# Position bias: the first layer of odd groups as table sums on GpSimd, with half the position columns

## What is computed

```python
pos = grid_q[:, :, None, :] - grid_kv[:, None, :, :]       # 1024 queries x 64 keys x (x, y)
bias = jnp.sign(pos) * jnp.log1p(jnp.abs(pos))
bias = jax.nn.relu(bias @ cpb_w1 + cpb_b1)                 # 2 -> 128
bias = jax.nn.relu(bias @ cpb_w2 + cpb_b2)                 # 128 -> 128
bias = (bias @ cpb_w3 + cpb_b3).reshape(b, GROUPS, H * W, Hd * Wd)   # 128 -> 1
```

## Time and profile before

| | us |
|---|---|
| median of 3 runs | 4444.17 (4442.83 to 4444.26) |
| the profiled execution | 4446.68 |
| its span, first to last instruction | 4444.9 |
| TensorE busy in the span | 3982.6 |
| VectorE, ScalarE, GpSimd busy | 2928.8, 2561.6, 1204.6 |
| bias stage, from 178 to 2381 us | 2203 |
| granted TensorE clock: span, bias stage | 0.942, 1.00 |

### The profile page before, as it was taken

The page is one execution under the profiler, slowest core; times in us unless marked ns, Lnnn a source line. Parts: engine busy times, 40 slices in busy tenths (PEclk is TensorE's granted clock), DMA queues, the critical chain, the costliest instruction groups (busy, mean ns, idle before and its releaser), DMA issues. The chain is left out here.

```text
span 4444.9 us, 65433 instructions
## 1 busy us (share of the span) xinstructions
PE 3982.6 (90%) x19500; PEld 2414.2 (54%) x19500; DVE 2928.8 (66%) x4207; ACT 2561.6 (58%) x4583; POOL 1204.6 (27%) x833
## 2 busy tenths in 40 slices
PE   2599999999999999999998999888778566969999
PEld 1355555555555555555556777747666442435553
DVE  7777777777777777777776233365888844235552
ACT  2488888888888888888885333322112330113331
POOL 1411111111111111111110554405676610026663
PEclk7799999999999999999999999999889777989999
DMA  1200000000000000000002000028999921363311
GB/s 44 87 2 2 2 2 2 2 2 2 2 2 2 2 2 2 2 2 2 2 2 77 1 0 0 17 76 299 369 369 375 363 88 51 129 151 67 67 39 76
DMA packets 136116, 309.14 MB, mean 70 GB/s; under 512 B 43400, under 2 KB 44424, under 8 KB 135004
## 3 DMA queue, kind: packets, MB, share of 16 engines
q1 hardware_dynamic: 94556, 157.02, 11.3%
q0 software_dynamic: 41472, 151.01, 8.7%
HBM read 228.83 MB, written 78.91 MB: 69 GB/s over the span
## 5 line engine op out<-in xcount | busy, mean ns | idle before, releaser
L572 DVE SCALAR_TENSOR_TENSOR cpb_r<-cpb_z,cpb_r 128x512 fp32r<-128x512 f32 x2052 | 1322.7, 687 | 491.5 <-ACT cpb_r L547 485.9
L547 ACT ACTIVATE cpb_r<-cpb_z 128x512 fp32r<-128x512 f32 x2052 | 1120.7, 604 | 280.0 <-PE cpb_z L479 280.0
L553 ACT ACTIVATE cpb_h<-cpb_z,net_vec 128x512 f32<-128x512 f32 x1536 | 1020.2, 713 | 1.8 <-PE cpb_z L495 1.8
L492 PE MATMUL cpb_z<-cpb_r,cpb_w2a 128*128 128x512 f32 x2048 | 856.7, 418 | 3.1
L493 PE MATMUL cpb_z<-cpb_r,cpb_w2b 128*128 128x512 f32 x2048 | 804.3, 393 | 0.0
L495 PE MATMUL cpb_z<-cpb_r,cpb_w2a 128*128 128x512 f32 x2048 | 798.2, 390 | 0.0
L430 POOL TENSOR_TENSOR cpb_exp<-l0k_posx,l0k_pos 128x1024 bf16 (+1 forms) x130 | 247.4, 1904 | 1968.8 <-PE cpb_z L479 1949.4
L492 PEld LDWEIGHTS cpb_z<-cpb_r,cpb_w2a 128*128 128x128 f32 x2048 | 384.1, 188 | 190.6 <-issue 123.4
L1405 DVE SCALAR_TENSOR_TENSOR dc_acc<-dc_g,dc_wt,dc_acc 128x512 f32<-128x512 f32 x560 | 444.8, 800 | 58.8 <-DMA dc_g<-conv_out,dc_idx 38.9
L504 PE MATMUL cpb_zo<-cpb_h,cpb_w3w 128*32 128x512 f32 x3584 | 477.3, 605 | 0.0
L495 PEld LDWEIGHTS cpb_z<-cpb_r,cpb_w2a 128*128 128x128 f32 x2048 | 385.2, 188 | 85.5
(11 more groups left out here) (331 smaller groups left out, 4910.7 us busy)
## 6 DMA issues: line engine op xcount, KB each, us to landing
conv_out<-dc_ys SPq DMA_DIRECT2D x576, 64.0 KB
qk_parts<-gn_r SPq DMA_DIRECT2D x64, 256.0 KB, 2.0
dc_wr<-in_dc_wT SPq DMA_DIRECT2D x9, 1024.0 KB
bias_dram<-cpb_bst SPq DMA_DIRECT2D x520, 8.0 KB
net_x<-in_x SPq DMA_DIRECT2D x8, 1024.0 KB, 8.8
sa_qa<-qk_parts SPq DMA_DIRECT2D x16, 512.0 KB
sa_ka<-qk_parts SPq DMA_DIRECT2D x16, 512.0 KB
dc_g<-conv_out,dc_idx POOLq DMA_INDIRECT x288
```

What stands on the lines that cost most here:

```text
L492: pe.matmul(z2[:, bank, :], W2A[:], R1[:, k, :], start=True, stop=False)
L547: act.activation(R1[:, t % RING, :], z1[:, t % 4, :], ACT.Relu).then_inc(r1_ready, 1)
L553: act.activation(H2[:, t % 8, :], z2[:, t % 3, :], ACT.Relu, bias=V("cpb_b2")).then_inc(h2a, 1)
L572: v.scalar_tensor_tensor(R2[:, t % RING, :], z1[:, t % 4, :], 0.0, R1[:, t % RING, :].bitcast(F32), ALU.max, ALU.subtract).then_inc(r2_rea ...
```

## The change

The first layer of odd quads is no longer a matmul. For their keys the logarithms go out to DRAM in f32 once (`log_dram`), and for each iteration SyncE loads them back, the same 512 numbers in all 128 partitions (LOG). VectorE makes tables (`table`): TAB[.., 0, x] = fx(x) w1[0] + b1 and TAB[.., 1, y] = fy(y) w1[1], 128 x (4 x 32) per operation, two operations for each of two slots. GpSimd adds them (`sums`): SUM[:, r, :] for 16 rows x 32 columns of queries, 128x512 f32, four for a quad, with both inputs read from TAB in broadcast. ScalarE and VectorE read SUM where they read z1 before. SUM has four slots, so the sums of the next odd quad wait until R2 of the last is made. POS holds only the keys of even quads, 64 groups in place of 128, and EXP is spread for one half of the queries at a time. Since the waits through z1 fall away in odd quads, ScalarE waits there for the sum of each tile and for z2.

```diff
+            sp.wait_ge(pos_step, 6)
+            for slot in range(2):
+                for r in range(4):
+                    for a in range(2):
+                        row = 32 * r + 16 * slot + 8 * a + 6
+                        sp.dma_start(g["log_dram"].rearrange("i s r a x -> s r a i x")[slot, r, a].unsqueeze(0),
+                                     U[0][row:row + 1]).then_inc(log_out, 16)
+            sp.wait_ge(log_out, 16 * 16)
...
-            v.tensor_tensor(U[0], gq.unsqueeze(1).broadcast_to([P, P, 32]),
-                            NTB.unsqueeze(2).broadcast_to([P, P, 32]), ALU.subtract).then_inc(pos_step, 1)
+            v.tensor_tensor(U[0], gq.unsqueeze(1).broadcast_to([P, GS, 32]),
+                            NTB.unsqueeze(2).broadcast_to([P, GS, 32]), ALU.subtract).then_inc(pos_step, 1)
...
-                    v.tensor_tensor(U[0], U[0], UB[:], ALU.subtract).then_inc(pos_step, 1)
+                    v.tensor_tensor(U[1], rest, UB[:], ALU.subtract).then_inc(pos_step, 1)
...
+            k, odd = divmod(quad, 2)
+            if odd:
+                slot, half = divmod(k, 2)
+                return half, slot, slot * 2 + 1
+            half, j = divmod(k, 2)
+            return half, j, j * 2
+
+        def on_pe(t):
+            return t // 4 % 2 == 0
+
+        def first_layer(t):
+            return z1[:, t % 4, :] if on_pe(t) else SUM[:, t % 4, :]
...
+                sp.wait_ge(tables, i * 2 + 4)
+                logs(bass.ds((i + 2) % ITERS, 1))
...
+            def sums(quad, table_count):
+
+                half, slot, _ = quad_of(quad % QUADS)
+                pool.wait_ge(table_step, table_count)
+                pool.wait_ge(tables, table_count)
+                for r in range(4):
+                    pool.tensor_tensor(SUM[:, r, :].rearrange("p (y x) -> p y x", x=W),
+                                       TAB[:, slot, r, 0, :].unsqueeze(1).broadcast_to([P, NF // W, W]),
+                                       TAB[:, slot, r, 1, half * 16:half * 16 + 16].unsqueeze(2).broadcast_to([P, NF // W, W]),
+                                       ALU.add).then_inc(sum_ready, 1)
...
-                    pe.wait_ge(r2_ready, i * TPI + quad * 4 + 8)
-                    layer1((quad + 2) % QUADS)
+                    if quad % 2 == 0:
+                        if quad + 2 == QUADS // 2:
+                            pe.wait_ge(exp_ready, i * 2 + 2)
+                        if quad + 2 == QUADS:
+                            pe.wait_ge(exp_ready, i * 2 + 3)
+                        layer1((quad + 2) % QUADS)
...
-                if t % 4 == 0:
-                    act.wait_ge(z1_ready, i * QUADS + t // 4 + 1)
-                act.activation(R1[:, t % RING, :], z1[:, t % 4, :], ACT.Relu).then_inc(r1_ready, 1)
+                if not on_pe(t):
+                    act.wait_ge(sum_ready, i * (TPI // 2) + t // 8 * 4 + t % 4 + 1)
+                    act.wait_ge(z2_ready, i * TPI + t + 1)
+                elif t % 4 == 0:
+                    act.wait_ge(z1_ready, i * (QUADS // 2) + t // 8 + 1)
+                act.activation(R1[:, t % RING, :], first_layer(t), ACT.Relu).then_inc(r1_ready, 1)
...
-                v.scalar_tensor_tensor(R2[:, t % RING, :], z1[:, t % 4, :], 0.0, R1[:, t % RING, :].bitcast(F32),
+                v.scalar_tensor_tensor(R2[:, t % RING, :], first_layer(t), 0.0, R1[:, t % RING, :].bitcast(F32),
...
+            def table(slot):
+
+                v.tensor_scalar(TAB[:, slot, :, 0, :], LOG[:, slot, :, 0, :], V("cpb_w1", 0), V("cpb_b1"),
+                                ALU.mult, ALU.add).then_inc(table_step, 1)
+                v.tensor_scalar(TAB[:, slot, :, 1, :], LOG[:, slot, :, 1, :], V("cpb_w1", 1), None, ALU.mult
+                                ).then_inc(tables, 1)
...
+                        if k == 3 and t in (16, 24):
+
+                            v.wait_ge(sum_ready, i * (TPI // 2) + (t // 8 - 1) * 8)
+                            v.wait_ge(log_in, i * 16 + 32)
+                            table(t // 8 - 2)
                         second_part(i, t + 4 + k)
```

More of the change, by code:

```diff
@@ L25 @@
 NJ = 64
+KPI = 16
 HID = 4 * C
@@ L340, in _ @@
             for part in range(3):
+                rest = U[min(part, 1)]
                 v.wait_ge(pos_step, n)
-                v.tensor_copy(UB[:], U[0]).then_inc(pos_step, 1)
+                v.tensor_copy(UB[:], rest).then_inc(pos_step, 1)
                 n += 1
@@ L422, in quad_of, with spread @@
         def quad_of(quad):
[L425 to L432, removed]
+            k, odd = divmod(quad, 2)
[8 more added lines that the diff above has]
+            return z1[:, t % 4, :] if on_pe(t) else SUM[:, t % 4, :]
+        def spread(eng, group, half):
+            rows = NF // W
+            eng.tensor_tensor(EXP[:, half].rearrange("p (y x) -> p y x", x=W),
+                              POSX[:, group, :].broadcast_to([P, rows, W]),
+                              POS[:, group, half * rows:half * rows + rows].rearrange("p o y -> p y o").broadcast_to([P, rows, W]),
                               ALU.add).then_inc(exp_ready, 1)
@@ L458, in _ @@
         def _(pool):
-            for slot in range(2):
-                spread(pool, slice(slot, slot + 1), slot)
+            def sums(quad, table_count):
[7 more added lines that the diff above has]
+                                       ALU.add).then_inc(sum_ready, 1)
+            for half in range(2):
+                spread(pool, slice(0, 1), half)
             pool.memset(W3W[:], 0.0).then_inc(win_zero, 1)
             pool.memset(H2[:, 4:8, :], 0.0).then_inc(win_zero, 1)
+            sums(1, 1)
             pool.sem_inc(stored, 16)
@@ L474, in layer1 @@
             def layer1(quad):
-                half, slot, j, _ = quad_of(quad)
+                half, j, _ = quad_of(quad)
                 for r in range(4):
                     rows = slice(32 * r, 32 * r + 32)
-                    mm = pe.matmul(z1[:, r, :], W1P[rows, j, :], EXP[rows, slot, half * NF:(half + 1) * NF],
+                    mm = pe.matmul(z1[:, r, :], W1P[rows, j, :], EXP[rows, half, :],
                                    start=True, stop=True)
@@ L501, in layer3 @@
                 pe.wait_ge(h2v, by_vector(i, quad * 4 + 3))
-                half, _, _, c = quad_of(quad)
+                half, _, c = quad_of(quad)
                 for r in range(4):
@@ L2210, in shape_columns @@
     group, half, axis, term = p // 32, (p // 16) % 2, (p // 8) % 2, p % 8
-    j8 = group + 4 * half
+    key = 8 * half + 4 * (term == 6) + group
     u_of = np.array([0, 1, 2, 0, 1, 0, 9, 9])
@@ L2221, in shape_columns @@
             one[:, None],
-            np.stack([j8 == k for k in range(8)], 1).astype(f),
+            np.stack([key == k for k in range(KPI)], 1).astype(f),
             np.stack([half == k for k in range(2)], 1).astype(f),
```

70 lines of the change are left out of this document (44 added, 26 removed).

## The result

The changed kernel takes 4365.5 us (median of 4 runs, 4365.0 to 4366.6) against 4443.5 us (median of 4 runs, 4438.8 to 4444.3) for the kernel before in the same job: a ratio of 0.9823, 95% interval 0.9811 to 0.9835, or 78 us less. The forecast was 4379 us with a range of 4325 to 4455. The profiled execution has a span of 4364.8 us at a mean granted clock of 0.944; before it was 4444.9 us.

What follows compares the result with a forecast made beforehand. The prediction took a ring of GpSimd's sums and VectorE's R2 to bound the bias stage at 33.5 us per iteration: -49, sampling -18, start +2, sum -65 from 4446.7, as a median 4379 us, range 4325 to 4455.

Steps and rivals of the forecast that it cites:

- TensorE: Bias stage: four removed first-layer groups give back 0.33 us each, 1.3 us per iteration, leaving TensorE alone needing 33.0 us.
- the 0.11 us stretch: Bias stage: first L492 takes 0.34 us where the next gap is 0.23; expected to stay, else 0.44 gained per group.
- The price of a sum: GpSimd's 128x512 f32 add for odd quads, taken as 1277 ns from L1954; four sums 5.0 us.
- Rival 1: Bias stage: TensorE stays the bound, with sums at 0.95 to 1.2 us or R2 slipping in free; 4345 us, chance 0.36.
- The ring: Bias stage: GpSimd's sums and the R2 that read them wait for each other; with spreads and tables, 33.5 us per iteration.
- some 0.5 us per iteration for H2 or R2: Bias stage: TensorE waiting this long, while VectorE waits for nobody, was among the signs that the forecast was right.
- So R2 doesn't hold L479: Bias stage before the change: VectorE's R2 doesn't delay the first-layer matmul; TensorE runs back to back and sets 34.27 us.
- Collisions: Bias stage: odd R2 with two SBUF inputs stand until GpSimd's sum ends; four R2 after the fourth sum take 2.6 us.
- Sampling: Before the bias stage: 35.8 us of position work in the chain to the interpolation matmul halves, -18 us.
- Start: Start of the bias stage: tables and four sums come ahead of or between the casts of the weights, +2 us.
- Tables, loads, stores: Tables add 0.9 us per iteration to the ring; SyncE's loads are hidden; the 16 logarithm stores fit before the bias stage.
- Twice a VectorE operation: Bias stage: a GpSimd sum of 1.50 us makes the ring 37.2 us per iteration and the time 4614 us; chance 0.03.

Runs made afterwards that it cites:

- the reordered kernel: The changed kernel with VectorE's H2 of an iteration's last quad put ahead of the last of the four R2 in that block: 4339.7 us, ratio 0.9763.
- the two runs: The changed kernel with every sum made twice and a wait for R2 before the first layer, 5072.3 us; the same with odd-quad R2 reading PSUM, 4745.9 us.

## Why the prediction was right in sign and 14 us too high

**TensorE: right.** The prediction took 4 x 0.33 = 1.3 us from an iteration; the pairs give 4 x 0.33, and the 0.11 us stretch stayed, behind L562. Forecast 33.0, measured 32.86 without the wait at the turn.

**The price of a sum: the step that failed.** "Nearest in size and type is L1954, 1277 ns; I take it." A sum takes 1.049 us. With operands that are full tiles, as L1954's are, it takes 1.29, so the size and type were a good match and the broadcast of the operands was the difference. The prediction had that the other way round: as a doubt that could only cost. Rival 1 had "Sums at 0.95 to 1.2 us" for the reason that "L430 needs 0.95 per 512 elements with the same broadcast pattern", and that was the better row.

**The ring: right as worked out, and not the bound.** At 1.29 us its 33.5 stands against an iteration of 33.3 and a ring that by itself is some 33.1 (the estimate above); no lap is off by more than 0.13. At 1.049, four sums are 4.07 us (a step of 1.02) and the same working gives 4 x (4.1 + 2.6) + 2 x 1.04 + 0.9 = 29.8, 3 us under TensorE, an estimate. TensorE stayed the bound, with a wait at the turn of the loop.

**What took the ring's place was in no rival.** The iteration is 33.31, not rival 1's 33.0: at the turn of the loop TensorE waits 0.45 us for the H2 of tile 30. The prediction said what would show the ring: TensorE waiting "some 0.5 us per iteration for H2 or R2". That sign came, from another cause; what gave it away is that GpSimd idles 3.8 us per pair, where the ring's working leaves it 2.6 (with full operands it idles 662 us, 2.6 per pair). That 33.31 came so near the forecast's 33.5 is in part luck: a stall that the prediction didn't have stood in for a ring that didn't bind. Rival 1's mechanism was the nearer one, and its 4345 would have been near the reordered kernel (4340).

**"So R2 doesn't hold L479": right, but one quad in eight is not like the one shown.** 34.27 is 8 x 4.267 + 0.13, and the 0.13 was this same wait for H2, which "TensorE runs back to back" left out.

**Collisions:** fewer than forecast, since most R2 begin after the sums. One odd R2 in 16 is over 0.75 us in the trace after; the forecast had them in every pair. **Sampling:** -18, measured -18.9; the sampling matmul was to start near 138 and starts at 137.3. **Start:** +2, measured +1.0. **Tables, loads, stores:** nothing, as forecast at this load.

**Twice a VectorE operation,** 4614 us: not so. Here a sum of 1.05 us stands beside a VectorE operation with two SBUF inputs of 0.69, a ratio of 1.5; with full operands (1.29) it is 1.9. What decides isn't the ratio but that GpSimd has 3.8 us to spare in each pair. The Trainium skill, GPSIMD Engine Reference, section Engine selection, says that two-input elementwise work takes about twice as long on GpSimd. The sums from full operands agree with it (1.9), the broadcast ones are better (1.5).

## What to carry to other kernels

Before taking "the engine runs back to back" from one period, divide the loop's whole time by its periods: what is left over is a stall at the turn, and it grows by all that a faster engine saves there. Work out a ring of engines lap by lap with its price per operation, then ask at which price it passes the bound; here that price lay between 1.05 and 1.29 us, and the tables, free on one side, cost 31 us on the other. When a change frees a buffer (here z1 in odd quads), look again at orders that it ruled out: moving one H2 gave 26 us more, and lost 33 us without the change.

## What the runs showed of the hardware

GpSimd adds two f32 operands into 128x512 in 1.049 us when both are read in broadcast from small tables, and in 1.29 us when both are full tiles. The prediction expected broadcast to cost or to be neutral; why it is faster isn't shown.

A VectorE operation with two SBUF inputs and a GpSimd add take turns, and either can be the one that stands: up to 1586 ns for one of 0.68, up to 1512 for one of 1.05. With the sums doubled, this is 326 us of the kernel; at the change's own load it costs TensorE nothing. The Trainium skill, SBUF — State Buffer, section Who interferes with whom, says that the two exclude each other; the two runs agree (326 us).
